# A four-layer network on one core: two expert layers that begin inside the stage before them

## What is computed, cut to what matters

```python
# layer 0: 3x3 conv to q, k, v; attention over a 7x7 neighbourhood, 8 heads of 16; 3x3 conv out
x = x + conv_out(neighbourhood_attention(conv_qkv(group_norm(ln(x)))))
# layer 1 (top 2 of 8 experts), layer 3 (top 1 of 8), layer 7 (top 2 of 8, gated)
t = t + sum_over_picked_experts(weight[e] * (act(norm(t) @ w1[e] + b1[e]) @ w2[e] + b2[e]))
# layer 2: full attention over the 2304 positions of an image, head size 16 (cut), values of 128
x = x + softmax(q @ k.T) @ v
```

## Time and profile before

| | |
|---|---|
| median of three runs | 1940.2 us |
| the profiled execution's own time | 1950.94 us |
| its span, first to last instruction | 1949.1 us |
| TensorE (PE) busy | 1480.9 us, 76% |
| VectorE (DVE) busy | 967.4 us, 50% |
| ScalarE (ACT) busy | 766.3 us, 39% |
| GpSimd (POOL) busy | 532.9 us, 27% |
| mean granted TensorE clock | 0.872 |

### The profile page before, as it was taken

How to read it: one execution, slowest core, us unless ns; L and a number is a source line. 1 busy time by engine, 2 the same in 40 slices (tenths; PEclk the granted TensorE clock), 3 DMA queues, 4 the chain that set the end, 5 groups by cost and what they waited for, 6 DMA issues and landing times. The chain is left out here.

```text
span 1949.1 us, 33422 instructions
## 1 busy us (share of the span) xinstructions
PE 1480.9 (76%) x10240; PEld 1356.2 (70%) x10240; DVE 967.4 (50%) x2689; ACT 766.3 (39%) x2083; POOL 532.9 (27%) x680
## 2 busy tenths in 40 slices
PE   3899998889955899917899996696439548369880
PEld 2799988888955899814798996686239324258870
DVE  6555555554152534426655554332561675654561
ACT  4211133333044865517344444553440442444440
POOL 2200045544023454340000001433220000346544
PEclk8899998987985999959899998798669769679995
DMA  6100000000051233210000001232000000023432
GB/s 211 37 1 1 7 15 21 23 20 20 1 207 48 81 113 96 73 38 1 1 1 1 1 0 75 75 89 69 10 0 0 1 0 0 21 77 116 116 90 86
DMA packets 103945, 89.83 MB, mean 46 GB/s; under 512 B 12120, under 2 KB 96100, under 8 KB 102384
## 3 DMA queue, kind: packets, MB, share of 16 engines
q1 hardware_dynamic: 92272, 64.28, 10.7%
q0 software_dynamic: 11520, 23.62, 4.1%
HBM read 46.43 MB, written 36.70 MB: 43 GB/s over the span
## 5 line engine op out<-in xcount | busy, mean ns | idle before, releaser
L1178 POOL DMA_INDIRECT slots<-U,m_slot_at x180 | 176.5, 981 | 381.2 <-DVE m_slot_at L1083 166.8
L896 PE MATMUL m_pre<-m_xg,m_own 128*128 128x128 f32 x1888 | 258.4, 281 | 14.1 <-DVE m_h L1133 4.5
L896 PEld LDWEIGHTS m_pre<-m_xg,m_own 128*128 128x128 f32 x1888 | 237.3, 197 | 16.8 <-ACT m_xg L982 9.1
L993 ACT ACTIVATE m_h<-m_pre,m_own 128x128 f32<-128x128 f32 x572 | 163.7, 375 | 76.0 <-PE m_pre L896 68.6
L1360 PE MATMUL at_mixed<-at_v,at_probs 128*128 128x130 f32 x1296 | 176.7, 275 | 0.0
L1360 PEld LDWEIGHTS at_mixed<-at_v,at_probs 128*128 128x128 f32 x1296 | 172.7, 191 | 4.6
L908 PE MATMUL m_out<-out_a,m_h 128*128 x1116 | 160.6, 281 | 10.2 <-DVE m_h L1133 9.4
L1405 ACT ACTIVATE at_probs<-at_scores 128x384 f32<-128x384 f32 x216 | 105.3, 490 | 152.6 <-PE at_scores L1375 151.7
L908 PEld LDWEIGHTS m_out<-out_a,m_h 128*128 128x128 f32 x1116 | 141.6, 194 | 15.8 <-issue 14.8
L1417 DVE TENSOR_REDUCE at_peaks<-at_sampled 128x1 f32<-128x512 f32 (+1 forms) x180 | 113.3, 637 | 59.1 <-PE at_sampled L1343 58.6
L1187 POOL DMA_INDIRECT U<-results,m_slot_at x108 | 103.2, 956 | 136.6 <-DMA results<-m_y 67.5
(11 more groups left out here) (328 smaller groups left out, 3423.3 us busy)
## 6 DMA issues: line engine op xcount, KB each, us to landing
m_x_in<-slots SPq DMA_DIRECT2D x62, 256.0 KB
results<-m_y SPq DMA_DIRECT2D x62, 256.0 KB
slots<-zeros SPq DMA_DIRECT2D x3, 2048.0 KB, 13.1
l_queries<-l_parts SPq DMA_DIRECT2D x256, 18.0 KB, 1.8
slots<-U,m_slot_at POOLq DMA_INDIRECT x180
X<-in_x SPq DMA_DIRECT2D x1, 2304.0 KB, 9.8
out<-X SPq DMA_DIRECT2D x1, 2304.0 KB, 7.0
in_a<-in_w SPq DMA_DIRECT2D x1, 2064.0 KB, 8.2
```

What stands on the lines that cost most here:

```text
L896: last = pe.matmul(pre[n % 2][:, c * 128:(c + 1) * 128], own[n % RING][:, c * 128:(c + 1) * 128], xg[n % RING][:, :], start=True, stop=True)
L993: last = act.activation(h[n % HELD][:, c * 128:(c + 1) * 128], pre[n % 2][:, c * 128:(c + 1) * 128], act_func, bias=own[n % RING][:, HID + ...
L1178: pool.indirect_dma_start(slots[b], bass.IndirectOffsetOnAxis(ap=slot_at[b][k][:, n:n + 1], axis=0), tokens[b][:, n, :], None).then_inc(la ...
```

## The change

It makes three moves.

1. In layer 0's attention there are three query buffers (`QS = 3`); queries are split two strips ahead (`split_queries(k + 2)`); the buffers' layout puts both parts of a head together, so that a DMA writes one run of 1152 bytes a partition for two of 576. The third buffer takes the place of the first convolution's squares and factors, so POOL clears it after the last scaling and before the first keys.
2. `mixture` no longer runs at once: it returns programs for the five engines that another stage can run up to a planned time (`alongside`), and `finish` runs the rest. In layer 1 two of three parts are judged, and the folding and 19 of 24 sends of part 0 are ordered, inside the out-convolution; its weights load there, the next layer's weights (in_b) in the expert loop. In layer 3 one of two parts is judged and sent inside the second image of layer 2. For that the second image is written out instead of looped, its sampling keeps one bank of two, and the other serves the judging.
3. Turning back (TensorE, line 923) is planned 8 instead of 4 after the fetch in all parts but the last, and some planned times inside the judging shift, in layer 7 too, where the exponentials of a part now stand before the next part's roots.

The diff, cut to its core:

```diff
+    QS = 3
...
+            with ExitStack() as released:
+                squares = [released.enter_context(nc.sbuf_tensor(f"l0_squares{m}", [128, TR, W], F32, side="right")) for m in range(2)]
...
+            queries = [of_early(f"queries{k}", [128, NH, 2, QY * W], F32R) for k in reversed(range(QS))][::-1]
...
+        following, loads = follow(Lead(2, 11.6, 5.8, 2, END, 0, 1.3, fold_at=27.0), x_ready)
+        following.banks(mixed, turned_o)
...
-                    if k < 2:
+                    if k < QS:
                         sp.wait_ge(zeroed[k], 1)
                     else:
-                        sp.wait_ge(scored, (k - 1) * UPS)
+                        sp.wait_ge(scored, (k - QS + 1) * UPS)
...
+                sp.wait_ge(o_turned, UNITS)
+                for target, source, arrived in loads:
+                    sp.dma_start(target, source).then_inc(arrived, 16)
...
+                for m in range(2):
+                    pool.wait_ge(scaled[m], NT)
+                pool.memset(queries[QS - 1][:, :, :, :].bitcast(F32), 0.0).then_inc(zeroed[QS - 1], 1)
                 for n in range(HELD):
                     stage(n)
+                split_queries(2)
...
-                    if n % UPS == 1 and k + 1 < STRIPS:
-                        split_queries(k + 1)
+                    if n % UPS == 1 and k + 2 < STRIPS:
+                        split_queries(k + 2)
...
+                following.engines.gpsimd.run(END)
...
+                def convolutions():
+                    for t in range(NT):
+                        yield 5.8 * t
+                        convolve_out(t)
+
+                following.engines.tensor.alongside(convolutions(), END)
...
+class Programs:
...
+    def run(self, until=math.inf):
+
+        while self.due:
+            entry = min(self.due, key=lambda entry: entry[0:2])
+            if entry[0] >= until:
+                return
+            self.due.remove(entry)
+            self.advance(*entry[1:])
+
+    def alongside(self, program, until):
+
+        for time in program:
+            self.run(min(time, until))
+        self.run(until)
...
+    norm_at = [lead.norm_at + TP * lead.gap * b for b in range(led)] + [(lead.end + 1.0 if lead else 0.0) + 26.0 * b for b in range(parts - led)]
+    gap = [lead.gap] * led + [1.0] * (parts - led) if lead else [1.0] * parts
+    judged_at = [norm_at[b] + TP * gap[b] for b in range(parts)]
+    sent_at = judged_at[0] + 11.0
+    send_gap = lead.send_gap if lead else 1.3
+    expert_at = [(lead.end + 5.0 if lead else 26.0 + SENT) + tiles * COST * b for b in range(parts)]
+    weights_at = [judged_at[b] + (8.5 if lead else 16.0) for b in range(parts)]
...
+                if n >= turned_banks:
+                    pe.wait_ge(rows_copied, n - turned_banks + 1)
...
+                yield fetched_at(b, i + 1) + (4 if b == parts - 1 else 8)
...
+        def load():
+            yield lead.end if lead else 0.0
+            for n, (target, source, arrived) in enumerate(loads):
+                yield lead.end + 16.0 * n + 20.0 if lead else 0.0
+                sp.dma_start(target, source).then_inc(arrived, 16)
...
+        PERIOD, STEP = 25.0, 1.33
+        END = PERIOD * GS
...
+        def bank_of(u, piece, alone):
+
+            return sampled[1 if alone else (u + piece) % 2]
...
+        def send_paced(engine, move):
+            engine.wait_ge(scored, (GROUPS + 2) * KC + 2 * move - 2)
+
+        following = follow(Lead(1, PERIOD * GROUPS + 12, 4.0, 1, END, 10, 2 * STEP), x_ready, send_paced)
+        following.banks([sampled[0], sampled[0]], [])
...
-                    pe.wait_ge(sampled_used, number + 1)
+                    pe.wait_ge(sampled_used, number + (2 if alone else 1))
```

More of the change, by code:

```diff
@@ L1230, in attention @@
-def attention(nc, P, XN, X):
+    s = Stage(nc, name)
+    both = range(parts)
+    outputs = 2 if second else 1
+    XIN, RING, HELD = 3, 4, 3
+    tokens = [room[:, :, :].rearrange("p r w -> p (r w)")[:, b * NP * C:(b + 1) * NP * C].rearrange("p (n c) -> p n c", c=C) for b in both]
+    rows, others, stats, total, apart, squared, var, shifted, inv_var, rstd, scale, shift = ({} for _ in range(12))
+    logits, below_peak, left, near, place, pick, peak, best, behind, summed, weight, counted = ({} for _ in range(12))
@@ new lines, in mixture, with allocate @@
+    tiles_of, starts, ends, lower, slot, slot_at, past, passed, code, codes = ({} for _ in range(10))
+    x_in, xg, own, gated, h, y, turned, x_turned, pre, out = ([] for _ in range(10))
+    def allocate(b, sb):
+        rows[b] = sb(f"{name}_rows{b}", [128, NP, JUDGED])
+        if top == 2:
+            others[b] = sb(f"{name}_others{b}", [128, NP, C])
+        stats[b] = sb(f"{name}_stats{b}", [128, NP, 6])
+        total[b], apart[b], squared[b], var[b], shifted[b], inv_var[b], best[b], behind[b], summed[b] = (
+            sb(f"{name}_{n}{b}", [128, NP]) for n in ("total", "apart", "squared", "var", "shifted", "inv_var", "best", "behind", "summed"))
+        rstd[b], scale[b], shift[b] = ([sb(f"{name}_{n}{m}{b}", [128, NP]) for m in range(outputs)] for n in ("rstd", "scale", "shift"))
+        logits[b], below_peak[b], left[b], near[b], place[b] = (
+            sb(f"{name}_{n}{b}", [128, NP, E]) for n in ("logits", "below_peak", "left", "near", "place"))
+        pick[b] = [sb(f"{name}_pick{k}{b}", [128, NP, E]) for k in range(top)]
+        peak[b], weight[b], slot[b] = ([sb(f"{name}_{n}{k}{b}", [128, NP]) for k in range(top)] for n in ("peak", "weight", "slot"))
+        slot_at[b] = [sb(f"{name}_slot_at{k}{b}", [128, NP], I32) for k in range(top)]
+        counted[b] = sb(f"{name}_counted{b}", [128, NP + 1, E], BF16)
+        tiles_of[b], starts[b], ends[b] = (sb(f"{name}_{n}{b}", [128, E]) for n in ("tiles_of", "starts", "ends"))
+        lower[b] = sb(f"{name}_lower{b}", [128, E, E])
+        past[b] = sb(f"{name}_past{b}", [1, groups * G, E])
+        passed[b] = sb(f"{name}_passed{b}", [1, groups * G])
+        code[b] = sb(f"{name}_code{b}", [1, groups])
+        codes[b] = sb(f"{name}_codes{b}", [1, groups], I32)
@@ new lines, in placed, with of_group, until, expert_of @@
+    def placed(b):
+        return (out[1] if apart_placed(b) else turned[0])[:, 0:(NP + 1) * E]
+    def of_group(tensor, i):
+        return tensor[i * G * 128:(i + 1) * G * 128, :].rearrange("(a p) c -> p a c", p=128)
+    def until(g):
+        return g // groups * tiles + min((g % groups + 1) * G, tiles)
+    def expert_of(engine, b):
+        held = {}
+        def load(m):
+            g = m // G
+            if g not in held:
+                held.clear()
+                held[g] = engine.value_load(codes[b][0:1, ds(g, 1)], min_val=0, max_val=E ** (2 * G) - 1)
+        def expert(m):
+            first = next(iter(held))
+            return (held[first] >> (3 * (m - first * G))) & (E - 1)
+        return load, expert
@@ L1240, in attention @@
+    return Mixture(allocate, banks, engines, finish)
+def attention(nc, P, XN, X, follow):
     KEYS = H * W
```

1001 lines of the change are left out of this document (523 added, 478 removed).

## The result

The changed kernel takes 1896.9 us, the median of four runs (1894.3 to 1900.4); the kernel before takes 1939.8 (1938.9 to 1940.3). The ratio is 0.978, 95% interval 0.977 to 0.980: 43 us faster. The forecast was 1868 with a range of 1844 to 1894, so the direction was right and the gain too large by 29 us, 3 beyond the range's end. The profiled execution after takes 1894.3 us with a span of 1892.5, so between the two profiles lie 56.6 us.

What follows compares the result with a forecast made beforehand. Time to win lay in query-DMA holes in layer 0's strip attention and idle heads of expert stages. From profiled 1950.9, 42 + 37 + 6 - 2 = 83, or from median 1940.2, 42 + 26 + 6 - 2 = 72: 1868 us, range 1844 to 1894.

Steps and rivals of the forecast that it cites:

- Part 1, the buffers: Layer 0's strip attention: three query buffers and earlier splitting remove the query wait and lowered clock; gain 42 us, bounds 25 and 50.
- the 7.5 us charged for GpSimd's wait and half clock: Strip attention: 4 us for POOL waiting on ACT over 31 strips, 3.5 us for two units at half clock.
- Rival B: Strip attention: POOL's wait for ACT costs 0.5 us a strip, so the buffers gain 20; 1890 us; chance 0.13.
- Part 2, layer 1's head: First expert stage begun beside the out-convolution: first expert matmul after 94.6 us for 131.8; gain 37, or 26 against the median.
- 81, and that is the stage's end, POOL's, not PE's: Out-convolution stage: 19 sends from 56.7 at 1.27 us each end it at 81; PE alone would end at 75.
- I put the 10.7 between them down to this crawl: Layer 1's slow folding matmuls: held to explain profiled 1950.9 against median 1940.2, so the head's gain was cut to 26.
- E: Out-convolution stage: its end waits for late-starting sends, so only 15 us is gained where 26 stood; 1879 us; chance 0.06.
- Part 3, layer 3's lead: Layer 3's experts begun in the attention's second image: head gains 37, experts lose 7, attention 37, turnings return 5; -2 us.
- A: Attention's second image: it pays less, so layer 3's lead gives +22 instead of -2; 1844 us; chance 0.15.
- C: Attention's second image: it pays more, bursts on ACT and DVE waiting for each other; -28; 1894 us; chance 0.14.
- Part 4, turnings: Expert loops of layers 1 and 7: later turning back removes waits for mixed tokens; 6 us beyond 5 counted for layer 3.
- ACT's tables: Table loads on ACT: 1.28 us each by the trace; the skill's 2.66 a switch would add 8, at most 3 on the path.

Runs made afterwards that it cites:

- e1: Kernel before with only the three query buffers and splitting two strips ahead, in the old layout; 1905.8 us, ratio 0.982.
- e2: Changed kernel with layer 3's judging and sending moved back behind the attention, which samples over both banks; 1886.0 us, ratio 0.971.
- e3: Changed kernel with layer 1's judging, folding and sending moved back behind the out-convolution, its weights still loaded beside it; 1901.0 us, ratio 0.978.
- e6: The changed kernel run again, unaltered, on chip 12; 1892.4 us, ratio 0.976.
- e7: Changed kernel with neither layer 1's nor layer 3's lead, keeping buffers, later turnings and shifted planned times; 1894.1 us, ratio 0.977.
- e9: Changed kernel without layer 3's lead, and with turning back planned 4 after the fetch in all parts, as before; 1892.4 us, ratio 0.976.
- e12: Changed kernel without layer 3's lead, repeated on chip 7; 1890.9 us, ratio 0.975.
- e13: The changed kernel run again, unaltered, on chip 7; 1897.8 us, ratio 0.979.
- e18: The changed kernel run again, unaltered, on chip 12; 1899.5 us, ratio 0.978.
- e19: Changed kernel without layer 3's lead, folding later, 24 unpaused sends beside the out-convolution, layer 3's fetches pausing; chip 12; 1885.0 us, ratio 0.971.
- e16: Changed kernel without layer 3's lead, but the attention's second image still sampling over one bank; chip 13; 1860.1 us, ratio 0.985.
- e8: Changed kernel without layer 3's lead, pausing after every four sends and, in expert loops, after each tile's fetches; 1891.5 us, ratio 0.975.
- e10: Changed kernel without layer 3's lead, folding later, 24 sends beside the out-convolution pausing after every four, layer 3's fetches pausing; 1866.3 us, ratio 0.963.
- e11: As e10, but pausing after every eight sends instead of four; 1874.0 us, ratio 0.967.
- e4: Changed kernel with none of layer 1's sends issued before the out-convolution ends, judging and folding staying in it; 1902.6 us, ratio 0.979.

## Why the prediction was wrong, by its own steps

**Part 1, the buffers: right between the profiles, 46 for 42.** The wait is gone and the clock is 0.99. The first score is 5.4 later (5 forecast). The strips take 51.7 less; of the 7.5 us charged for GpSimd's wait and half clock about 3 came (187.0 us from the first score to the last, for 183.4 of clean units). Rival B had no part in it. Against the median the part gives 36, with 42 still inside its interval of 27 to 45.

**Part 2, layer 1's head: the step that failed.** Forecast 94.6 us, measured 112.8; 19 us won in the profiles where 37 stood. The step is "81, and that is the stage's end, POOL's, not PE's", with PE done at 75. It let TensorE work at its full pace while 19 sends go out beside it. Measured, the last convolution matmul starts at 91 (539.7 against 448.6), because TensorE stands still for 12 to 13 us; then come the ranking of part 1, VectorE's chain and the last addition, and the barrier is passed at 97, where 82 stood. The sends themselves were done at 85 (532.3 + 0.96).

The earlier trace rows had the warning: 64 one-column matmuls in 29 us. "I put the 10.7 between them down to this crawl" took it for an accident of one execution, instead of asking what ran beside it. It is in all twelve profiles outside chip 13 in which sends go out in one piece beside TensorE's folding or convolution (before, after, e1, e2, e3, e6, e7, e9, e12, e13, e18, e19), and the move carried it from an idle head into full convolutions.

On the chip without the standstill the same order (e16) gives a head of 103.5 us. So some 9 of the 18 us are the standstill's (9 to 11 by the other profiles of this order), and 9 are plain errors of the sum, which e16 shows: the sends start at 60.7, not 56.7, since part 0 is ranked at 56 and not at 53; the barrier takes 3.5 us after the last send is done, not 1, and the last of the five later sends starts at 94, not 87; from there to the first expert matmul it is 9.5 us, not 7.7, with 18 of part 2's judging matmuls in between, most of them at half clock. E was nearest in kind, and it named the late sends, but these are the smaller reason.

One cost had no term at all: with the lead, part 2's judging and normalising run among layer 1's first expert tiles, where they take 5 to 6 us (e3, e7). The forecast had such guests in layer 3 only.

The deduction of 10.7 from this part was wrong too, for e1, e3 and e7 have the crawl in profiled executions that lie within 3 us of their medians. It is not why 1868 was missed: by e1 those 10.7 us seem to belong to part 1, and taken off there they leave the sum as it is. That is luck.

**Part 3, layer 3's lead: the mechanism right, one term short.** Head 35.5 won (37 forecast). The attention pays 32.3 (37): 16.3 for the bank (16 forecast), 16 for the guests (21). The loop costs 12 where 7 for guests less 5 for turnings stood: the guests cost 9 to 10, and 2 to 4 remain without a lead of layer 3 (107.9, 108.9 and 106.1 in e2, e12 and e7 for 104.5), whose cause I haven't found. Sum -9 for -2, and undoing it alone won 7 us. It lies within the bounds that I gave, and what the forecast concluded, a lead that is worth nothing, was even kind. Rivals A and C wanted guests that cost the attention much less or much more, and neither came.

**Part 4, turnings: near in layer 1, wrong in layer 7.** They are worth 4 to 7 us in loop 1 (e9) for 5.4, but with the lead's guests the loop is only 3 shorter than before. In layer 3, where 5 stood, they bring 4.5 on the chip without standstill; on the others loop 3 is 2 to 3 us longer with them. In layer 7 nothing is seen.

**ACT's tables.** In the attention after, a load of 1.28 us starts at 1042.77, the root at 1044.29, the next load at 1044.52 and the exponential at 1045.82: 3.05 us for two switches with the root between. The Trainium skill, ScalarE: Activation LUTs, section What ACT_TABLE_LOAD costs, would have 5.3 for two; the trace keeps to the row, as the sum did. The last exponential before them ends at 1042.75, so there is no drain ahead of the first load either.

In sum: 46.3 + 19.1 - 8.9 + 0.1 for turnings and the rest = 56.6 between the profiles, for a forecast of 83.

## What to carry to other kernels

When work moves from an idle stage into a full one, everything slow in it moves too: a stretch that crawls in the profile has to be explained before it is moved, not put down to the profile. A lead is worth what it takes off a head less what it adds in both stages beside it; here a bank given up cost 16 of 35 us before any guest arrived. And when two engines end a stage together, freeing one of them (e8) shows nothing until the other is moved as well (e10).

## What the runs showed of the hardware

On chips 1, 7 and 12, and in both profiles shown first, indirect DMAs that GpSimd issues back to back, 1.26 us each, brought TensorE down to about one instruction in 0.7 to 1.4 us after eleven to eighteen of them, and VectorE with it, until 4 to 5 us after the last was issued. Waiting until every four had landed (1.5 to 3.2 us each time) removed it. Waiting after every eight did not quite: in e11 it began after the twelfth send, four after a wait. Without sends (e4) it did not appear in that place, and paced by TensorE's own progress, as in the attention, it was not there either. Among the convolutions a record of instruction loading lies within 2.5 us of each onset. But in the heads of before, e1, e3 and e7 the nearest one comes 5 to 8 us after it, and e4 and e10 have such records in the same stretch with no standstill. So loading alone is not the cause; what is, and why chip 13 is free of it (1891 us for the kernel before), stays open. Layer 3's loop has three tiles of 5.0, 5.2 and 3.8 us before and 4.2, 5.9 and 3.9 after beside eight fetches in one piece. With the pauses, on the same chips, no tile takes over 4.4 (e8, e10, e11, e19); on chip 13 none did beside twelve fetches in one piece either (e16).
